# A late page list, two page gathers in flight, masks and a low part on VectorE, norm factors between the gathers

## The reference, cut to what matters

```python
x = x + attn0(x @ weight[adapter_ids].T)          # small heads, one weight matrix per sequence
x = x + routed_ffn(lora(x))
x = x + attention1(gate(x))                       # 32 heads, 8 key/value heads, D = 128, distance bias
x = x + quantised_ffn(attention2(x, cached keys and values))
# attention 2, per sequence b and key/value head g (4 query heads each):
q, k = rope(rmsnorm(q, q_norm_w), pos), rope(rmsnorm(k, k_norm_w), pos)    # pos = cache_seqlens[b] + token
kc = k_cache[block_table].reshape(bsz, 512, HK, D)   # 16 pages of 32 tokens
k_all, v_all = concat([kc, k]), concat([vc, v])      # 512 cached + 128 own = 640 keys
valid_c = arange(512) < cache_seqlens[:, None]       # the key mask; own keys are always valid
o = softmax(where(valid, q @ k_all.T * scale, -1e30)) @ v_all
```

## Time and profile before

| | before |
|---|---|
| time, median of 3 runs | 2070.08 us (2068.37 to 2071.62) |
| time of the profiled execution | 2064.11 us |
| its span in the trace | 2062.0 us |
| granted TensorE clock, mean, as a share of full | 0.988 |
| busy: PE / DVE / ACT / POOL | 1971.8 / 1560.4 / 1315.9 / 942.1 us |

### The profile page before, as it was taken

The page is one execution under the profiler, slowest core; times in us unless marked ns, Lnnn a source line. Parts: engine busy times, 40 slices in busy tenths (PEclk is TensorE's granted clock), DMA queues, the critical chain, the costliest instruction groups (busy, mean ns, idle before and its releaser), DMA issues.

```text
span 2062.0 us, 35942 instructions
## 1 busy us (share of the span) xinstructions
PE 1971.8 (96%) x12214; PEld 1677.1 (81%) x12221; DVE 1560.4 (76%) x3384; ACT 1315.9 (64%) x3796; POOL 942.1 (46%) x926
## 2 busy tenths in 40 slices
PE   4999999999999999979999999999999999999987
...
GB/s 205 125 53 47 52 1 72 79 117 112 128 97 104 118 96 80 117 43 84 33 42 74 31 83 32 33 82 32 83 33 33 83 31 34 85 32 82 24 29 36
DMA packets 91158, 142.21 MB, mean 69 GB/s; under 512 B 24914, under 2 KB 63058, under 8 KB 86498
## 3 DMA queue, kind: packets, MB, share of 16 engines
...
## 4 chain that ended last, share of the span: by engine, by line
PE 76%; DVE 6%; POOL 5%; ACT 4%; DMA 4%; issue 4%; SPq 2%; ACTq 0%; DVEq 0%; POOLq 0%
PE PS L1721 9%; PE PS L1633 8%; PE PS L1733 8%; PE PS L1706 6%; PE PS L1688 6%; PE PS L1556 6%; PE PS L1499 6%; PE PS L1647 4%; PE PS L1691 3%; PE PS L344 3%; PE PS L1512 3%; POOL ffn_weights L1308 2%; PE PS L1527 2%; DMA ffn_weights<-in_kcache,arena 2%; PE PS L1542 2%
## 5 line engine op out<-in xcount | busy, mean ns | idle before, releaser
L1308 POOL DMA_INDIRECT ffn_weights<-in_kcache,arena x256 | 258.1, 1008 | 183.8 <-DVE ffn_weights L2047 72.7
L2593 POOL DMA_INDIRECT vcache<-in_vcache,rows x256 | 248.5, 971 | 83.1 <-issue 64.7
L2599 POOL TENSOR_TENSOR vcached_lo<-vcache,vcached_hi 128x512 fp32r<-128x512 f32 x64 | 83.2, 1300 | 392.4 <-ACT vcached_hi L2430 392.4
L2448 ACT ACTIVATE pr<-pr,sm 128x640 f32<-128x640 f32 x256 | 209.5, 821 | 66.2 <-DVE sm L2063 66.2
L2079 DVE TENSOR_TENSOR prT_lo<-PS,prT_hi 128x512 fp32r<-128x512 f32 x320 | 208.1, 682 | 30.2 <-ACT prT_hi L2459 30.2
L2459 ACT ACTIVATE prT_hi<-PS 128x512 fp32r<-128x512 f32 x320 | 178.0, 597 | 72.7 <-PE PS L1706 72.6
L2063 DVE CUSTOM_DVE_ANT_0 pr<-PS,ffn_weights,sm 128x640 f32<-128x640 f32 x256 | 210.8, 879 | 1.7 <-PE PS L1691 1.7
L1706 PE MATMUL PS<-consts,pr 128*128 128x128 f32 x1280 | 173.1, 273 | 4.7 <-DVE prT_lo L2079 3.7
L1706 PEld LDWEIGHTS PS<-consts,pr 128*128 128x128 f32 x1280 | 149.9, 141 | 29.5 <-DVE prT_lo L2079 5.3
L1688 PE MATMUL PS<-kT_hi,qT_hi 128*128 128x320 f32 x512 | 156.0, 313 | 7.3 <-DVE sm L2063 6.5
L1688 PE MATMUL PS<-kT_lo,qT_hi 128*128 128x320 f32 x512 | 154.4, 309 | 0.0
...
## 6 DMA issues: line engine op xcount, KB each, us to landing
...
```

Of the source, the lines that this page charges most:

```text
L1308: pool.indirect_dma_start(out=key_pages[:, n % 2, c, :], out_offset=None, in_=T["kcache"], in_offset=bass.IndirectOffsetOnAxis(ap=key_rows ...
L2448: act.activation(pr2[:, h, :], pr2[:, h, :], ACT.Exp, bias=nm2[:, h:h + 1], scale=-1.0, accum_out=rs2[:, h:h + 1]).then_inc(a2_ex, 1)
L2593: pool.indirect_dma_start(out=vcache[:, c, :], out_offset=None, in_=T["vcache"], in_offset=bass.IndirectOffsetOnAxis(ap=rows[:, g, b, c:c ...
```

## The change

Seven edits in the hand-written orders:

1. The four DMAs of `key_page_i` leave SP's start-up and are issued after the first alibi table; DVE makes `key_row0` from them just before `step1(4)`.
2. `key_pages_gathered` becomes two semaphores, one for each buffer, and a gather no longer waits for the landing of the one before.
3. The masks are made by DVE: the zeroes and the masks of sequences 0 and 1 at the end of `step1(63)`, mask i + 2 at the end of `step(i)`. `pool_masks` is gone.
4. A load of turned keys waits for its own item's store, not for all 64. `hi_of_cached_k(0)` of ACT goes from `step1(62)` to `step1(63)`. `lo_of_cached_k` goes from POOL to DVE, all 64 of them.
5. POOL makes the norm factors after the second of the four gathers. It takes over one weights' low part per group (part 2); DVE keeps parts 0, 1, 3 and 4.
6. SP loads the output weights of the next group at b = 3, not b = 2.
7. In the steps with q >= 2 (the last ones, with the feed-forward) DVE makes `lo_of_o(i - 1)` after the four row maxima, not before.

```diff
         def sp_paged_inputs(sp):
             for q in range(4):
                 sp.dma_start(page_i[q * 32:(q + 1) * 32, :], T["pages"][q, :].partition_broadcast(32)).then_inc(s_setup, 16)
-            for q in range(4):
-                sp.dma_start(key_page_i[q * 32:(q + 1) * 32, :],
-                             T["pages"].rearrange("c (b q) -> q (c b)", q=CHUNKS)[q, :].partition_broadcast(32),
-                             allow_slow_non_contiguous=True).then_inc(s_setup, 16)
             sp.dma_start(clen_i[:], T["cache_len"].partition_broadcast(P)).then_inc(s_setup, 16)
...
             def gather(n):
                 g, b = group_of(n)
                 wait(pool, s_kpt, n - 1)
-                wait(pool, s_kpg, 16 * CHUNKS * n)
                 for c in range(CHUNKS):
                     pool.indirect_dma_start(out=key_pages[:, n % 2, c, :], out_offset=None, in_=T["kcache"],
                                             in_offset=bass.IndirectOffsetOnAxis(ap=key_rows[:, g, c, b:b + 1], axis=0)
-                                            ).then_inc(s_kpg, 16)
+                                            ).then_inc(s_kpg[n % 2], 16)
...
-        def pool_masks(pool):
-
-            pool.wait_ge(s_kps, 16 * ITEMS)
-            for b in range(B):
-                pool.tensor_scalar(keymask[:, b, 0:CACHED], cst["iota"], clen[:, b:b + 1], -NEG,
-                                   ALU.is_ge, ALU.mult).then_inc(a2_mask, 1)
-                pool.memset(keymask[:, b, CACHED:NKEY], 0.0).then_inc(a2_mask, 1)
...
             table(0)
+            sp.wait_ge(s_setup, 16 * NSETUP + NROWS)
+            for q in range(4):
+                sp.dma_start(key_page_i[q * 32:(q + 1) * 32, :],
+                             T["pages"].rearrange("c (b q) -> q (c b)", q=CHUNKS)[q, :].partition_broadcast(32),
+                             allow_slow_non_contiguous=True).then_inc(s_setup, 16)
...
             def load_keys(n):
                 wait(sp, a2_kcl, n)
+                if n < ITEMS - 1:
+                    sp.wait_ge(s_kps, 16 * (n + 1))
...
             load_weights2(0)
-            sp.wait_ge(s_kps, 16 * ITEMS)
+            load_out_weights2(0)
...
                 elif i == ITEMS - 1:
+                    lo_of_cached_k(0)
                     lo_of_own_v(0)
...
                 for n in turns_in(i):
                     turn_keys(n)
+                if i == ITEMS - 1:
+                    own_masks()
+                    mask(0)
+                    mask(1)
...
+            def lo_of_cached_k(n):
+                dve.wait_ge(a2_kch, n + 1)
+                dve.tensor_tensor(kT2[1][:, 0:CACHED], kcache[:].rearrange("p c d -> p (c d)"), kT2[0][:, 0:CACHED],
+                                  ALU.subtract).then_inc(a2_kcl, 1)
...
+            def own_masks():
+                dve.wait_ge(s_kps, 16 * ITEMS)
+                dve.wait_ge(s_kpt, ITEMS)
+                ch.mark(dve.memset(keymask[:, :, CACHED:NKEY], 0.0))
+
+            def mask(b):
+                masked[b] = ch.mark(dve.tensor_scalar(keymask[:, b, 0:CACHED], cst["iota"], clen[:, b:b + 1], -NEG,
+                                                      ALU.is_ge, ALU.mult))
...
-                if i:
+                if i and q < 2:
                     lo_of_o(i - 1)
                 for h in range(GH):
                     row_max(i, h)
+                if q >= 2:
+                    lo_of_o(i - 1)
...
                 if more:
                     lo_of_q(i + 1)
+                    lo_of_cached_k(i + 1)
                 lo_of_probs(i, 2)
...
                 if new_weights:
+                    dve.wait_ge(a2_wl, QPARTS * (g + 1) + 3)
                     lo_of_weights(g + 1, 3)
...
                 if b == B - 3 and g < G - 1:
-                    for part in range(3):
+                    for part in range(2):
                         lo_of_weights(g + 1, part)
+                if i + 2 < B:
+                    mask(i + 2)
...
                 if i == ITEMS - 2:
                     hi_of_weights(0, KT)
-                    hi_of_cached_k(0)
                 if i == ITEMS - 1:
                     hi_of_own_v(0)
+                    hi_of_cached_k(0)
                     hi_of_q(0)
...
                 lo_of_cached_v(i)
                 if i + 1 < ITEMS:
-                    load_values(i + 1)
+                    load_values(i + 1, (0, 1))
                     factors(i + 1)
-                    lo_of_cached_k(i + 1)
+                    load_values(i + 1, (2, 3))
+                if i % B == B - 3 and i // B < G - 1:
+                    lo_of_weights(i // B + 1, 2)
```

41 lines of the change are left out of this document (26 added, 15 removed).

## The result

The changed kernel takes 2023.67 us in the median of 4 runs (2018.47 to 2024.67), the kernel before 2070.85 in 4 runs (2068.37 to 2072.77): ratio 0.9768, 95% interval 0.9748 to 0.9788, 47.2 us faster. The two profiled executions differ by less, 2064.11 and 2024.04, so 40.1 us: the one of before was 6.7 us faster than the median of its runs, the one of after stands among its own.

A forecast was written before the change was run, and what follows sets the result against it. PE was taken as the bound, busy 1971.8 of 2062.0 us, leaving some 90 us to gain. Terms of −16.5, −14, 0, −3, −1, −2.5 and 0 gave −37, from the 2070 median to 2033 us; range 2024 to 2056.

The forecast's parts named there:

- Two gathers in flight: Attention 1: POOL is on no path of PE that the rows show, so 0 us.
- Late page list: Start-up: SP issues the second sequence's input 13.8 to 17.6 us earlier, so −16.5 us, ends −13.5 and −18.5.
- Masks and keys: Between the attentions: PE's waits of 3.7 and 9.3 us go, clock stays up; −14 us, ends −10.5 and −16.3.
- The subtraction on DVE: Steps of attention 2: cached keys' low part adds 0.60 us, own key's multiplication saves 0.54; 0, ends 0 and +3.
- The 0.2 us to spare: Step of attention 2: about 0.2 us before PE's turnings need the third low part of the probabilities.
- Factors between the gathers: Steps of attention 2: two gathers less ahead of the factors shorten PE's waits; −3 us, ends 0 and −5.
- Group ends: Ends of groups: row-maximum waits of 1.6 us before the last 162 us shrink; −1 us, ends 0 and −1.6.
- Tail: From 1900 to 2000 us: row maxima start 0.6 us sooner, output's product waits longer; −2.5 us, ends 0 and −4.9.
- term 3: Steps of attention 2: moving the cached keys' low part from POOL to DVE costs and gains nothing, 0 us.
- A: Start-up: not set by SP's issuing, so gains only some 5 us; 2045 us in all, chance 0.13.
- B: Steps of attention 2: multiplication stays at 0.83 us, DVE's subtraction costs in full, +25 us; 2058 us, chance 0.14.
- C: Steps of attention 2: gathers hold DVE's multiplication, third low part comes late, +43 us; 2076 us, chance 0.06.

The follow-up runs named there:

- e2: Kernel before with the late page list alone (key_page_i loads behind the first alibi table, key_row0 just before step1(4)): 2065.98 us beside 2081.96, ratio 0.9924.
- e8: Changed kernel with the masks made by POOL again, after the last store: 2038.22 us beside 2019.96 of the changed kernel.
- e6: Kernel before with the cached keys' low part on DVE for items 1 to 63, nothing else: 2065.07 us beside 2066.86, ratio 0.999.
- e12: Repeat of e6, the kernel before with the cached keys' low part on DVE: 2066.36 us beside 2065.79, ratio 1.0005.
- e7: Changed kernel with the cached keys' low part on POOL again for items 1 to 63, behind the gathers: 2019.68 us beside 2019.96.
- e1: Kernel before, unchanged, run again on a chip slower for it: 2084.14 us beside 2081.96, ratio 1.0002.
- e11: Changed kernel with the norm factors behind all four gathers again: 2024.61 us, ratio 0.9799 to the kernel before.
- e9: Changed kernel with the output's low part ahead of the row maxima in the last steps again: 2021.76 us, ratio 0.9789 to the kernel before.
- e15: Changed kernel with each gather of key pages waiting again for the landing of the one before: 2027.42 us beside 2020.86 of the changed kernel.
- e16: Changed kernel, unchanged, run beside e15 on the same chip: 2020.86 us, ratio 0.976 to the kernel before.
- e13: Kernel before with two tiny POOL operations ahead of the cached keys' low part, so that it starts later: 2068.68 us beside 2071.86, ratio 0.9989.
- e14: Kernel before with the same two tiny POOL operations as e13, but the cached keys' low part on DVE: 2062.87 us beside 2071.86, ratio 0.9959.

## Why the prediction was wrong

The direction and most terms held; the step that failed is the last of the sum, "Two gathers in flight: 0", which measured 6.6 us, and with it the way from the profile to the median. With −6.6 in its place the sum gives 2026.5.

1. *Late page list, −16.5:* 16.0 (e2). Inside the term two errors cancel, which is luck: the restart gained 19.4, not 16.5, because the data came at once (a wait of 1.36 us) and the clock stayed up, and 3.7 went back because DVE lost the pause that hid its constants. I had not asked what else used PE's pause.
2. *Masks and keys, −14:* 14.9 in each of four traces. With the masks alone back, 14.7 of it is lost (e8), so the term wasn't a sum of two gains: the 3.7 us of L1527 are worth nothing while the masks stay on POOL.
3. *The subtraction on DVE, 0:* right on the chips that are like the profile (e6, e12, e7). The 0.2 us to spare was right too, and on one side of it the kernel before stood with no margin: with the third low part 0.4 us later in the step it loses 17 us (e1). One profile can't show that; a slack as thin as that should have gone into the range as a gain that the change might bring, beside the costs. L2036 fell to 0.40 us and not to 0.29, but held up nothing.
4. *Factors between the gathers, −3:* 3.1 to 3.3 in the traces (e11). It came by the waits for low parts alone, not by the own key's turning too.
5. *Group ends, −1:* no run undoes this part alone. Of the 1.6 us that I put ahead of the last steps, 0.4 lie behind 2000 us.
6. *Tail, −2.5:* 2.3 in the traces between 1840 and 2000 us, and 2.3 by the medians (e9), unsure there. The output's low part became a wait of its own, as the term had feared.
7. *Two gathers in flight, 0:* 6.6 (e15 and e16), 6.3 in the table of the result. The wait for it was in the profile, that of PE at L1534 (6.5 us in 4, the longest 4.8) that I left out of the earlier trace rows. I had seen that POOL waits for landings, and asked only whether PE waits for POOL in the rows, not how late the next gathers leave behind such a wait and what lies beside them then.

The profile's own sum was −37 and the profiles differ by 40.1. The rest of the 47.2 us, 7 us, is the distance of the first profile from its runs, which I carried over to the changed kernel as if it were a fixed offset. Between 1000 and 1840 us such a distance is seen in e1 and e13 as short waits for the third low part. In e14's set, whose kernel before took 2071.86 (here 2070.85), moving the subtraction to DVE was worth 9.0 us, so term 3 may well be where the 7 us are. That it is so on the first chip, whose unprofiled runs have no trace, is argued and not shown. The first profile is none of the runs beside it, and on which chip it was taken isn't on record; on a chip of e6's kind its 2064.11 would be an ordinary time.

Of the rivals, A, B and C are out: PE's wait is 1.36 us, the multiplication fell to 0.40 in the middle, and a gather delayed its end by 0.13 in the middle and held nothing behind it. The port rule of the Trainium skill ("SBUF — State Buffer", who interferes with whom) would have had DVE held by both. POOL's subtraction does hold it, 0.83 to 1.02 us where e6 without it has 0.28; behind a gather DVE's next instruction starts after 0.19 us in this kernel, and the measurement decides.
